# A decoder layer on one core: the split activations are given other start addresses in SBUF

## What is computed

```python
x = layernorm(x + self_attention(x, W_Q, W_K, W_V, W_out, b_out))
x = layernorm(x + cross_attention(layer_norm(x, ln_w, ln_b), ctx, Wq, Wkv, Wout, mask, 5))
gate, up = x @ wg.T, x @ wu.T            # wg, wu: int / 127, 768 x 256
x = layernorm(x + (silu(gate) * up) @ wd.T)
```

## The kernel before

| product (item in the order) | moving | loaded | matmuls a batch |
|---|---|---|---|
| queries and keys (Q, K) | xTs | wq, wk | 72 |
| values (V), 512 wide | wv | xTs | 12 |
| output of self-attention (OUT) | wo | Z | 48 |
| cross queries (XQ) | NX | xwq | 24 |
| cross values (XV), 512 wide | xwv | ctxs | 6 |
| output of cross-attention (XOUT) | xwo | H (its first 4 blocks) | 24 |
| gate and up (FFN) | NT | wg, wu | 72 |
| down (DOWN) | wd | H | 36 |

## Time and profile before

### The profile page before, as it was taken

The page is one execution under the profiler, slowest core; times in us unless marked ns, Lnnn a source line. Parts: engine busy times, 40 slices in busy tenths (PEclk is TensorE's granted clock), DMA queues, the critical chain, the costliest instruction groups (busy, mean ns, idle before and its releaser), DMA issues.

```text
span 2047.8 us, 50579 instructions
## 1 busy us (share of the span) xinstructions
PE 2012.4 (98%) x18166; PEld 1850.2 (90%) x18166; DVE 1540.0 (75%) x5708; ACT 1322.9 (65%) x3992; POOL 376.2 (18%) x624
## 2 busy tenths in 40 slices
PE   7999999999999999999999999999999999999997
PEld 6899999999999999999999999999999999999886
DVE  5777777777777777777777777777777777777764
ACT  7867666666666666666676666666666666666642
POOL 2111211211212121112111112112121211121211
PEclk9999999999999999999999999999999999999998
DMA  4100000000000000000000000000000000000000
GB/s 162 32 8 22 19 12 22 8 22 18 22 12 19 11 19 21 19 12 16 14 22 19 12 22 8 22 18 22 12 19 11 19 21 19 12 19 11 14 7 11
DMA packets 49607, 41.19 MB, mean 20 GB/s; under 512 B 19537, under 2 KB 47569, under 8 KB 49361
## 3 DMA queue, kind: packets, MB, share of 16 engines
q1 hardware_dynamic: 49360, 37.96, 6.4%
HBM read 29.56 MB, written 8.39 MB: 19 GB/s over the span
## 4 chain that ended last, share of the span: by engine, by line
PE 96%; DVE 1%; ACT 1%; issue 1%; SPq 0%; DMA 0%; POOL 0%; POOLq 0%; DVEq 0%; ACTq 0%
PE gen L441 20%; PE gen L443 19%; PE gen L442 19%; PE s_ps L581 9%; PE z_ps L623 7%; PE gen L529 3%; PE pt_ps L602 3%; PE gen L542 3%; PE gen L538 3%; PE z_ps L625 3%; PE pt_ps L603 3%; PE pt_ps L607 3%; PE gen L509 2%; PE gen L500 1%; PE gen L553 1%
## 5 line engine op out<-in xcount | busy, mean ns | idle before, releaser
L947 ACT ACTIVATE SM<-SM,least 128x128 f32<-128x128 f32 (+1 forms) x1024 | 452.4, 447 | 35.5 <-DVE least L1474 35.5
L877 ACT ACTIVATE PT<-pt_ps 128x512 f32<-128x512 f32 (+1 forms) x512 | 237.4, 486 | 235.8 <-PE pt_ps L603 234.2
L1474 DVE CUSTOM_DVE_ANT_0 SM<-s_ps,causal 128x128 f32<-128x128 f32 (+1 forms) x1024 | 314.0, 352 | 27.9 <-PE s_ps L581 21.3
L1487 DVE TENSOR_SCALAR SM<-SM,total 128x128 f32<-128x128 f32 (+1 forms) x1024 | 280.2, 336 | 9.1
L1855 POOL TENSOR_TENSOR H_lo<-gated,H_hi 128x256 fp32r<-128x256 f32 x192 | 141.3, 743 | 511.1 <-ACT H_hi L877 511.0
L930 ACT ACTIVATE gated<-gen 128x256 f32<-128x256 f32 x192 | 73.7, 384 | 213.2 <-PE gen L443 213.0
L581 PE MATMUL s_ps<-KT,QT 64*128 64x128 f32 (+1 forms) x2048 | 202.9, 337 | 0.6 <-ACT KT L877 0.6
L947 ACT ACTIVATION_READ_ACCUMULATOR SM<-SM,least 128x1 f32 x1024 | 197.1, 192 | 0.0
L1451 DVE SCALAR_TENSOR_TENSOR gated<-gated,gen 128x256 f32<-128x256 f32 x192 | 80.9, 421 | 121.0 <-ACT gated L930 120.8
L623 PE MATMUL z_ps<-PT,Vt 128*64 128x256 f32 x1024 | 168.2, 399 | 0.0
L581 PEld LDWEIGHTS s_ps<-KT,QT 64*128 64x128 f32 x2048 | 148.6, 189 | 21.3 <-issue 7.2
(11 more groups left out here) (185 smaller groups left out, 6508.4 us busy)
## 6 DMA issues: line engine op xcount, KB each, us to landing
xT_in<-in_xT SPq DMA_DIRECT2D x32, 256.0 KB, 2.9
x_in<-in_x SPq DMA_DIRECT2D x32, 256.0 KB, 2.8
out<-rows SPq DMA_DIRECT2D x32, 256.0 KB, 2.2
ctx_in<-in_ctxT SPq DMA_DIRECT2D x32, 77.0 KB, 2.8
mask_in<-in_maskT SPq DMA_DIRECT2D x32, 77.0 KB, 2.6
SX<-in_wq SPq DMA_DIRECT2D x1, 512.0 KB, 7.1
rows<-in_wv SPq DMA_DIRECT2D x1, 512.0 KB, 8.0
xwk<-in_xwkv SPq DMA_DIRECT2D x1, 512.0 KB, 8.2
```

The lines of the kernel that those rows point to most:

```text
L877: return act.activation(o, i, ACT.Copy)
L947: ins = act.activation(part, part, ACT.Exp, scale=-1.0, bias=least[:, i % 4, n:n + 1], accum_out=total[:, i % 4, n:n + 1])
L1474: ins = dve.tensor_tensor_reduce(SM[:, i % 4, at:at + keys], s_ps[bank][:, col:col + keys], causal[:, S - keys:S], -SCALE, -3 * NEG, ALU.a ...
L1487: ins = dve.tensor_scalar(part, part, total[:, i % 4, n:n + 1], None, ALU.mult)
```

## The change

`halves_at` reserves 32 elements (128 bytes) more than a tensor needs and starts it `ahead` bytes from a 128-byte step within that room: `ahead // 4 % 32` elements in, which is 28 elements (112 bytes) for -16, 30 elements (120 bytes) for -8 and 4 elements (16 bytes) for 16. `xTs`, `Z`, `NX`, `NT` and `H` are made with it. `ones`, `minus_half` and `eps` move from ahead of `x_in` to behind `H`, and `H` moves up to them.

```diff
+        def halves_at(name, n, ahead):
+
+            a = ahead // 4 % 32
+            return [sb(name + part, [P, n * S + 32], F32R)[:, a:a + n * S].rearrange("p (n s) -> p n s", n=n)
+                    for part in ("_hi", "_lo")]
...
         causal = sb("causal", [P, S])
-        ones = sb("ones", [P, 1])
-        minus_half = sb("minus_half", [P, T])
-        eps = sb("eps", [P, T])
...
-        xT_s = halves("xTs", [P, KD, S])
+        xT_s = halves_at("xTs", KD, -16)
...
-        Z_s = halves("Z", [P, NP, S])
+        Z_s = halves_at("Z", NP, -16)
...
-        NX_s = halves("NX", [P, KD, S])
-        NT_s = halves("NT", [P, KD, S])
+        NX_s = halves_at("NX", KD, -8)
+        NT_s = halves_at("NT", KD, 16)
+        H_s = halves_at("H", KH, 16)
+        ones = sb("ones", [P, 1])
+        minus_half = sb("minus_half", [P, T])
+        eps = sb("eps", [P, T])
...
-        H_s = halves("H", [P, KH, S])
```

## The result

The changed kernel takes 2058.34 us (median of 5 runs, 2057.27 to 2060.35) against 2048.26 us for the kernel before (5 runs). The ratio is 1.0051, with a 95% interval of 1.004 to 1.0063: slower by half a per cent, where 2027 us was forecast.

What follows compares the result with a forecast made beforehand. The prediction took TensorE's matmul-to-matmul pace as the bound, TensorE being busy for 98% of the span. Its terms summed to 697 ns a batch, times 32 batches 22.3 us, less 1 us: 2027 us, range 2012 to 2047 us.

Steps and rivals of the forecast that it cites:

- Everything that went from 32 to 64 beside the five: Transposes, KT with QT, PT with Vt, ScalarE's copies and small constants: essentially 0 ns, copies no more than 8 ns.
- the value for an unmeasured distance: Split products at 48, 56 or 80 apart were given the mean pace seen at 64, 114.5 ns.
- Q and K: xTs as moving operand, 72 matmuls a batch from 117.9 to 114.5: 245 ns saved, bounds 0 and 310.
- OUT: Z loaded, 48 matmuls a batch from 118.5 to 114.5: 192 ns saved, bounds 0 and 235.
- FFN: NT moving, 72 matmuls a batch from 116.7 to 114.5: 158 ns saved, bounds -130 and 223.
- XQ: NX moving, 24 matmuls a batch from 117.5 to 114.5: 72 ns saved, bounds -24 and 94.
- V: xTs loaded, 512 wide, 12 matmuls a batch from 234.5 to 232: 30 ns saved, bounds 0 and 88.
- H: DOWN and XOUT, H from 64 to 80: taken at 0, bounds 54 ns gain and 240 ns loss.
- The fourth: Exactly 64 apart is needed: DOWN and XOUT lose 240 ns a batch, others stay, 2056 us; chance 0.09.
- Rivals 1 and 3: 1: all runs settle at the fast pace, 2017 us, chance 0.21. 3: addresses have no effect, 2048.5 us, chance 0.11.
- Rival 2: Only the loaded side counts; only OUT and V gain, 2041 us; chance 0.17 together with other partial gains.
- the forecast of 114.5 ns for all: Pace for 256-wide split products: mean of DOWN at 113.6 and XOUT at 115.85, slow runs included.

Runs made afterwards that it cites:

- the control: The kernel before with the five split activations moved behind all other tensors, each offset from a 512-byte line kept; 2047.75 us, ratio 1.000.

## Why the prediction was wrong

**What held.** TensorE's pace is the whole matter: no wait, engine or clock changed, and the paces account for the loss. DOWN is fast because of the 64 bytes: moving H alone by 16 costs it 5.1 ns a matmul. The distance, not the place, counts (everything shifted by 64: no change). XOUT's alternation comes from ctx_in, as was inferred from the earlier trace rows. Everything that went from 32 to 64 beside the five was free, though `ones` is read by VectorE and not by GpSimd as the prediction has it. The rule of the Trainium skill, "TensorE: Matmul & The Clock Gate", section on what each phase of a matmul is for, that loading the next weights steals no read bandwidth from the running matmul gives no room for any of this. The measurement decides against it: 21 us lie between the control and the kernel with all at 0, which differ in addresses alone. What no run shows is how the stream and the load get in each other's way, or whether that is the cause at all; shown is only that their distance matters.

**The step that failed** is the value for an unmeasured distance: "I take for them what 64 gives in the trace", for 48, 56 and 80. No row had such a distance, and I put them near 64 because they are near in bytes. The effect has no such neighbourhood. At 60 and 68 the fast pace is gone, and at 48, 56, 72 and 80 too. The terms that stood on it:
- Q and K: -245 ns a batch forecast, -22 measured. OUT: -192, and it was +58. FFN: -158, and +137. XQ: -72, and +53. V: -30, and -55, the only gain of the size forecast or more.
- H: taken at 0, measured +158 for DOWN and +48 for XOUT, within the bound of 240 that was given for the loss.
- The bounds themselves were too narrow on the losing side. OUT's was 0, on the argument that 118.5 was the slow pace. But 118.5 was only the slow pace at 32: FFN reaches 118.9, OUT 119.6 and XQ 119.7 in the changed kernel, 120 at distance 0 and 121 at 60. The rows showed 64 and, on two sides, 32, and nothing of what other distances cost.
- The halves: the prediction took a tensor as one place. The 128 spare bytes of `halves_at` put the low half 128 bytes further round than the high one, and with H back at exactly 64 this alone kept DOWN at 118.8. So this edit could not have kept DOWN's pace even at 64.

**The rivals.** The fourth, exactly 64 apart is needed, is what happened, with 2056 us priced and 2058 measured. It was given 0.09, and the range stopped short of it. That its price came out near is in part luck, for its errors pull both ways: it left out that FFN, XQ and OUT would lose as well (248 ns), took more from H (240 for 206), and took nothing for the gain of V and of Q and K (77). It had 240 ns a batch where the paces gave 377. Nor is 64 the only distance with a fast pace: XQ at 16 and Q and K at 112 reached it in some runs, which neither this rival nor the forecast had. What spoke for it stood in the prediction already. XOUT took two paces with the same addresses, so the fast one is a state that is easily missed. A step as sharp as 113.6 against 117.8, with nothing between, is the mark of a state that either holds or not, and such a state is not a value to interpolate. The two cases should have had about equal chances. Rivals 1 and 3 fall with DOWN, which lost its pace to 16 bytes. Rival 2, that only the loaded side counts, falls with FFN, which streams its activation: 117.0 before, 118.9 in the changed kernel, 114.5 at exactly 64. (Its upper bound is 2038 us by its own terms, not 2037.)

**A second step that was incomplete.** Even at exactly 64 the forecast of 114.5 ns for all was too good: with all five there the mean was 115.6 to 117.6, because the pace into which a run settles depends on the product ahead of it. The prediction counted half of XOUT's turns as slow, which was the right kind of allowance, but treated the entry as a matter of one product, where each product depends on the one ahead, and a fast one can be the reason for a slow one behind it.

## What to carry to other kernels

In a kernel that is bound by back-to-back matmuls, read the pace from start to start in each product, and if products of one shape differ, compare the distance between their streamed and loaded operands in SBUF modulo 128 bytes, and the offset of the high and low halves modulo 256. Change it in a step of its own and read each product's pace rather than the total: the gain of one is easily eaten by the next, whose pace depends on it. And where a trace shows two sharp levels and nothing between, don't price a point near the good one at the good level: take the good and the bad one as two cases.

## What the runs showed that was not expected

- With float32r operands and 256 columns, runs of matmuls hold 113.3 or 117.8 ns steadily at a distance of 64 bytes, 120 at 0, and wander between about 115 and 123 at 32 (OUT, mean 118.4) and at 96 (Q and K, mean 118.1). None of the kernels showed a steady pace below 113.3 for this shape.
- What runs ahead decides the pace of a whole product: DOWN's over 36 matmuls depended on the offset of xTs, which it doesn't read, and XOUT's over 24 on the half of ctx_in that the cross keys had streamed. It can also turn it over: with all at 64, a slow FFN led to a fast OUT in 15 turns and a fast one to a slow OUT in 14.
- Nearer to 64 was slower, with equal halves: OUT 119.5 ns at 60 against 117.7 at 48, FFN 120.4 at 56 against 117.9 at 48, XQ 121.1 at 60 against 120.0 at 72.
- Two good distances for the two halves don't make a good pair: with 192 and 320 modulo 512 DOWN ran at 118.8, with either for both at 113.7 to 113.9.
- V, with 512 columns, fell from 234.2 to 229.6 to 230.7 at distances of 0, 48 and, with xTs at 320, 64; with xTs at 448, also 64, it stayed at 233.3.
